# Four output tiles of the seventh image set among the eighth image's norm instead of its energies, in an attention kernel on one core

## The chip, the cores and the metric

The kernel runs on one core of one Trainium2 chip. The metric is the device time of the whole program in microseconds, the median of several runs. The engines are TensorE (PE, matmuls), VectorE (DVE), ScalarE (ACT), GpSimd (POOL) and SyncE (SP, which only issues DMAs here).

## What is computed

The input `x` holds 8 images of 32 x 32 tokens with 256 channels, in float32. Two layers are added to it, each on a group norm without weights (32 groups of 8 channels, mean and variance over the image and the group):

```
x = x + L0(gn(x))        # 8 heads of 32; attention within each row of 32 tokens; projection and bias
x = x + L1(gn(x))        # one head over all 1024 tokens of an image

L1:  q = x Wq, k = x Wk   (256 -> 32)      v = x Wv   (256 -> 256)
     energy = k q^T       (1024 x 1024)    attn = softmax(energy, rows)
     L1 = gamma * (attn v)
```

## The kernel before

Work is told by image. Stage `a` is L0 (norm, q, k, v, scores within windows, softmax, output, projection), stage `b` is L1. A float32 operand is carried as a high and a low float16 half, and a product is three matmuls (high by high, high by low, low by high: `split3`, L274 to L276).

Stage `b` of an image has these steps. The norm (`transposes`, `group_mean`, `group_var`, `group_scale`, then `normalise` on ScalarE and `b_norm_split` on VectorE, which makes the halves) is followed by q and k (`b_project_qk`, L561), whose halves are stacked by four DMAs (`b_stacks`, L332). `b_energy(it)` (L581) computes 128 rows of energies into the two PSUM banks `pb[0]` and `pb[1]`, and `b_maximum` (L1032) takes their row maxima. Energy `it` waits for maximum `it - 1`, since the banks are the same. With all eight maxima there, `b_max_split`, `b_max_rows` and `b_rows_in` put them into the stacks, and `b_energy_T(jt)` (L600) computes the transposed energies less the maximum, again in `pb[0:2]`. ScalarE takes the exponential (L832, L833) and VectorE makes its low half (`b_exp_low`, L1044, semaphore `b_el`). An output tile `b_output(it)` (L611) sums over the eight `jt` the product of exponentials and `v`: 24 matmuls of 257 columns, of which the last column is the sum of the row. `b_factor` (L1051, two small instructions) makes the tile's factor from that sum, `b_scaled` (L835) scales the tile into `y_part`, which has two places and shares its memory with `qk_h`, `b_add` (L1243) adds it to the residual, and `store_pair` (L296) stores two tiles at a time.

The order is written out by hand for every engine, as two half steps per image, `first(i)` and `second(i)`, run one after the other by `all_steps` (L236); images 2 to 4 are a hardware loop, and the others are written out with plain integers. An engine takes its instructions strictly in this order, and a semaphore wait holds up all that is queued behind it on that engine.

- `first(i)` holds on TensorE the outputs of image `i - 1` (L632), eight tiles, and among them the energies of image `i`, and stage `a` of later images where there is one. For i = 7 there is no such image, so it holds the outputs of image 6 and the energies of image 7 alone.
- `second(i)` holds the transposed energies of image `i` and, where they exist, the output projection and the norm and q/k of image `i + 1` (L663).
- The last image is already treated apart (`last_image`, L278): its outputs 0 to 5 are computed `jt` by `jt` inside `second(7)` (`outputs_behind`, L654), into six banks, and only tiles 6 and 7 are left for `first(8)`, which reuse the banks of tiles 0 and 1 and so wait for their scaling (`b_part`).
- `result_bank` (L281) says which bank a tile uses. Images other than the last use `pb[2]` and `pb[3]` in turn, so that tile `it` waits until tile `it - 2` was scaled. The banks `pa[0:4]` belong to stage `a`.
- On VectorE (L1058) each `b_factor` of image `i - 1` stands among the maxima of image `i`. In `second` (L1086) the instructions of the norm's `group_mean` are followed by `b_exp_low(i, 7)`, and that by `group_scale`.

Of the kernel before, what the change touches and what calls it, by code (L numbers as in the profile page):

```python
# [36 lines left out]
IMAGES, TOKENS, CH = 8, 1024, 256  # L37
# [14 lines left out]
def nth(b, per, n):  # L52
    return b * per + n


def build(nc, x, w_qkv, w_proj, b_proj, wq1, wk1, wv1, gamma, ident_d, group_d, masks_d, out):
# [3 lines left out]
    with ExitStack() as ctx:  # L60
# [81 lines left out]
        pa = ctx.enter_context(nc.psum_tensor("pa", [P, 4, CHUNK], F32))  # L142
# [39 lines left out]
        a_ol = sem("a_ol")  # L182
# [95 lines left out]
        def last_image(b):  # L278
            return isinstance(b, int) and b == IMAGES - 1

        def result_bank(b, it):  # L281

            if last_image(b):
                it = it % 6
                return pa[:, it, :] if it < 4 else pb[:, it - 2, :]
            return pb[:, 2 + it % 2, :]

        def out_banks(g):
# [118 lines left out]
        def _(pe):  # L407
# [50 lines left out]
            def a_project_qk(b, c, ds):  # L458
                for d in ds:
                    pe.wait_ge(n_["a"]["nl"], nth(b, 4, 2 * c + 2))  # L460


                    if c == 0 and image(b, 1):
                        pe.wait_ge(a_sub, 1 + d // 2)
                    elif c == 0:
                        after(pe, a_ol, nth(b, 2, 0))
                    elif d < 2:
                        pe.wait_ge(a_qe, nth(b, 4, d + 1))
                    elif isinstance(b, int) and b < 2:
                        pe.wait_ge(a_ke, nth(b, 4, d - 1))  # L470
                    else:
                        pe.wait_ge(a_x1, nth(b, 4, d - 3))
                    project_T(pa[:, d, :], wqkv_h, wqkv_l, slice(d * P, (d + 1) * P), c, a_nh, a_nl).then_inc(a_qk, 1)
# [126 lines left out]
            def b_energy_T(b, jt):  # L600

                if jt == 0:
                    pe.wait_ge(b_rows, nth(b, 1, 1))
                else:
                    pe.wait_ge(b_exp, nth(b, 8, jt))
                for c in range(CHUNKS):
                    last = nc.tensor.matmul(pb[:, c, :], q_stack[0:98, jt * P:(jt + 1) * P],  # L607
                                            k_stack[0:98, c * CHUNK:(c + 1) * CHUNK], start=True, stop=True)
                last.then_inc(b_st, 1)

            def b_output(b, it, b_next, jts=range(TILES)):  # L611

                if last_image(b):
                    pe.wait_ge(b_el, nth(b, 8, jts[-1] + 1))

                    if it >= 6:
                        pe.wait_ge(b_part, nth(b, 8, it - 5))
                elif jts[0] == 0:
                    pe.wait_ge(b_el, nth(b, 8, 8))

                    if it >= 2:
                        pe.wait_ge(b_part, nth(b, 8, it - 1))
                    else:
                        pe.wait_ge(b_vl, nth(b, 4, 4))
                rows = slice(it * P, (it + 1) * P)
                for jt in jts:
                    last = split3(result_bank(b, it)[:, 0:CH + 1], (e_h[:, jt, rows], e_l[:, jt, rows]),
                                  (v_h[:, jt, 0:CH + 1], v_l[:, jt, 0:CH + 1]), start=(jt == 0), stop=(jt == TILES - 1))
                if jts[-1] == TILES - 1:
                    last.then_inc(b_pv, 1)  # L630

            def first(i, b, o, m, f):  # L632

                for it in range(4):
                    if o and not last_image(i - 1): b_output(i - 1, it, b, range(0, 4))
                    if b and it == 2: b_energy(i, 1, m)
                    if o and not last_image(i - 1): b_output(i - 1, it, b, range(4, 8))
                    if f and it == 1: transposes("a", i + 2, range(4))
                    if b and it >= 1: b_energy(i, (0, 2, 3)[it - 1], m)
                for it in range(4, 8):  # L640
                    if o and last_image(i - 1):

                        if it >= 6: b_output(i - 1, it, b)
                        continue
                    if o: b_output(i - 1, it, b, range(0, 4))
                    if m and it == 5: a_output(i + 1, f, 0)
                    if f and it == 5: group_var("a", i + 2)
                    if m and it == 6: a_output(i + 1, f, 1)
                    if b and it == 7: b_energy(i, it, m)
                    if o: b_output(i - 1, it, b, range(4, 8))  # L650
                    if b and it < 7: b_energy(i, it, m)
                    if f and it == 4: group_mean("a", i + 2)

            def outputs_behind(b, jts):  # L654

                for jt in jts:
                    if jt == 0:

                        pe.wait_ge(b_vl, nth(b, 4, 4))
                    for it in range(6):  # L660
                        b_output(b, it, False, (jt,))

            def second(i, b, o, m, f):  # L663
                if b and not image(i, 0): b_project_v(i, (0,))
                if b: b_max_rows(i)
                if b and not image(i, 0): b_project_v(i, (1,))
                if b: b_energy_T(i, 0)
                if b and not image(i, 0): b_project_v(i, (2,))
                if f: a_project_qk(i + 2, 0, (0,))
                if b: b_energy_T(i, 1)  # L670
                if f: a_project_qk(i + 2, 0, (1,))
                if b and not f: b_project_v(i, (3,))
                if b: b_energy_T(i, 2)
                if f: a_project_qk(i + 2, 0, (2, 3))
                if b: b_energy_T(i, 3)
                if f: a_project_qk(i + 2, 1, (0,))
                if last_image(i): outputs_behind(i, (0,))
                if b: b_energy_T(i, 4)
                if b and f and not image(i, 0): b_project_v(i, (3,))
                if last_image(i): outputs_behind(i, (1,))  # L680
                if f: a_project_qk(i + 2, 1, (1,))
                if b: b_energy_T(i, 5)
                if last_image(i): outputs_behind(i, (2,))
                if m: a_projection(i + 1, f, (0, 1))
                if b: b_energy_T(i, 6)
                if last_image(i): outputs_behind(i, (3,))
                if m: a_projection(i + 1, f, (2,))
                if m: transposes("b", i + 1, (0, 1))
                if m: a_projection(i + 1, f, (3,))
                if b: b_energy_T(i, 7)  # L690
                if last_image(i): outputs_behind(i, range(4, 8))
                if f: a_project_qk(i + 2, 1, (2,))
                if f: a_project_qk(i + 2, 1, (3,))
                if m: transposes("b", i + 1, (2, 3))
                for j in range(4):
                    if m and j == 2: group_var("b", i + 1)
                    if f: a_project_v(i + 2, (j,))
                    if m and j == 0: group_mean("b", i + 1)
                if f: a_scores(i + 2)
                for c in range(CHUNKS):  # L700
                    if m: b_project_qk(i + 1, f, c)
# [228 lines left out]
        def _(dve):  # L930
# [126 lines left out]

            def first(i, b, o, m, f):  # L1058
                if m: a_maximum(i + 1, 1)
                if o: b_factor(i - 1, 0)  # L1060
                if m: a_row_sum(i + 1, 0)
                if b: b_maximum(i, 0)
                if o: b_factor(i - 1, 1)
                if m: a_row_sum(i + 1, 1)
                if b: b_maximum(i, 1)
                if o: b_factor(i - 1, 2)
                if m: a_transpose(i + 1, 0)
                if b: b_maximum(i, 2)
                if f: stats("a", i + 2, (0,))
                if b: b_maximum(i, 3)  # L1070
                if o: b_factor(i - 1, 3)
                if f: stats("a", i + 2, (1,))
                if m: a_transpose(i + 1, 1)
                if f: group_mean("a", i + 2)
                if o: b_factor(i - 1, 4)
                if b: b_maximum(i, 4)
                if f: group_scale("a", i + 2)
                if b: b_maximum(i, 5)
                if o: b_factor(i - 1, 5)
                if b: b_maximum(i, 6)  # L1080
                if o: b_factor(i - 1, 6)
                if b: b_maximum(i, 7)
                if b: b_max_split(i)
                if o: b_factor(i - 1, 7)
# [239 lines left out]
```

## Time and profile before

| | |
|---|---|
| median of 3 runs | 681.19 us (679.55 to 682.06) |
| the profiled execution, its own time | 680.34 us |
| its span, first to last instruction | 678.6 us |
| mean granted clock of TensorE | 0.947 of full |
| `second(6)` in it, by TensorE's first value projection to the last q/k matmul | 570.02 to 611.43 us |
| `first(7)` | 611.43 to 638.53 us |
| `second(7)` | 638.53 to 668.64 us |
| `first(8)`, the tail | 668.64 us to the end |

All times in rows are from the start of the span. The duration of a row for a matmul includes its way through the array; one matmul of a dense sequence starts long before the last has ended, so its price is the distance between starts. The granted clock (PEclk) is the mean in a stretch, as a share of 2.4 GHz; 0.50 is 1.2 GHz.

### The profile page before, as it was taken

How to read it: one execution, taken by the hardware profiler on the slowest of the kernel's cores; microseconds unless marked ns; L12 is line 12 of the kernel's file. 1: busy time of each engine (PE TensorE's matmuls, PEld its weight loads, DVE VectorE, ACT ScalarE, POOL GpSimd, SP SyncE). 2: the span in 40 equal slices, each digit the busy share in tenths (PEclk: the TensorE clock that was granted, in tenths of full speed). 3: DMA queues.
4: the chain of work that ended last, by engine and by line, in shares of the span. 5: the costliest groups of instructions: out<-in, count | busy, mean ns of one | idle time of the engine just before them, and what ended most of it. 6: DMA issues, size and time to landing. Idle time of an engine off the chain costs nothing.

```text
span 678.6 us, 15147 instructions
## 1 busy us (share of the span) xinstructions
PE 594.0 (88%) x5859; PEld 429.7 (63%) x5859; DVE 474.0 (70%) x765; ACT 349.0 (51%) x486; POOL 196.3 (29%) x194
## 2 busy tenths in 40 slices
PE   2797827699999999999999999999999999649987
PEld 2464714347776686767775777578676767427756
DVE  4553387567877888687868786887869784764562
ACT  2762233466438751885358643865188514641463
POOL 6432050403244204503351324321450242001303
PEclk8799878779999999999999999999999999779989
DMA  5222413034132232233224313223323132201101
GB/s 165 75 48 65 125 62 86 1 78 108 27 95 78 63 103 72 68 82 94 63 68 108 93 24 93 81 68 90 79 67 75 33 78 68 66 1 39 49 0 63
DMA packets 40308, 47.53 MB, mean 70 GB/s; under 512 B 6848, under 2 KB 32320, under 8 KB 40256
## 3 DMA queue, kind: packets, MB, share of 16 engines
q1 hardware_dynamic: 35792, 42.42, 23.9%
q10 hardware_dynamic: 4464, 4.39, 1.9%
q8 instruction: 35, 0.57, 0.4%
q14 instruction: 17, 0.14, 0.1%
HBM read 10.09 MB, written 8.39 MB: 27 GB/s over the span
## 4 chain that ended last, share of the span: by engine, by line
PE 67%; DVE 16%; ACT 7%; issue 5%; DMA 2%; SPq 2%; POOL 0%; DVEq 0%; ACTq 0%; POOLq 0%
PE pb L274 10%; PE pb L275 9%; PE pb L276 9%; PE pa L274 6%; PE pa L276 6%; PE pa L275 6%; PE pa L541 5%; PE pb L607 4%; DVE max_neg L1034 4%; PE pa L508 4%; PE pb L589 3%; PE pa L429 2%; DVE ast L936 2%; ACT e L833 2%; DVE bst L936 2%
## 5 line engine op out<-in xcount | busy, mean ns | idle before, releaser
L274 PE MATMUL pb<-v_h,e_h 128*128 128x257 f16 x464 | 127.4, 275 | 0.0
L276 PE MATMUL pb<-v_h,e_l 128*128 128x257 f16 x464 | 126.4, 272 | 0.0
L275 PE MATMUL pb<-v_l,e_h 128*128 128x257 f16 x464 | 126.1, 272 | 0.0
L1034 DVE TENSOR_REDUCE max_neg<-pb 128x1 f32<-128x1024 f32 x64 | 77.5, 1211 | 53.6 <-PE pb L589 53.2
L1049 DVE TENSOR_TENSOR e_l<-e,e_h 128x1024 f16<-128x1024 f32 x64 | 77.9, 1224 | 21.1 <-ACT e L833 19.6
L842 ACT ACTIVATE qk_h<-pb,y_fac 128x256 f32<-128x256 f32 x58 | 27.5, 474 | 109.9 <-DVE y_fac L1056 109.6
L1248 POOL TENSOR_TENSOR y<-qk_h,y 128x256 f32<-128x256 f32 x64 | 46.3, 726 | 117.7 <-ACT qk_h L842 117.6
L833 ACT ACTIVATE e<-pb,f_energy 128x1024 f32<-128x1024 f32 x64 | 71.3, 1114 | 16.7 <-PE pb L607 16.7
L1229 POOL TENSOR_TENSOR xb<-xin,bias 128x2048 f32<-128x2048 f32 x8 | 36.2, 4527 | 142.3 <-DVE x L1014 138.9
L1234 POOL TENSOR_TENSOR before_turn<-before_turn,a_rinv 128x1024 f32<-128x1024 f32 x16 | 30.7, 1922 | 93.0 <-DVE a_rinv L995 93.0
L832 ACT ACTIVATE e_h<-pb,f_energy 128x1024 f16<-128x1024 f32 x40 | 44.5, 1114 | 21.3 <-PE pb L607 21.3
L274 PEld LDWEIGHTS pb<-v_h,e_h 128*128 128x128 f16 x464 | 45.7, 99 | 13.6 <-issue 1.4
L275 PEld LDWEIGHTS pb<-v_l,e_h 128*128 128x128 f16 x464 | 45.6, 98 | 11.9
L589 PE MATMUL pb<-q_stack,k_stack 96*128 96x512 f16 x128 | 39.9, 394 | 15.0 <-DVE max_neg L1034 13.0
L274 PE MATMUL pa<-a_nh,wqkv_h 128*128 128x512 f16 x128 | 49.4, 386 | 2.7 <-DVE wqkv_l L1157 1.3
L607 PE MATMUL pb<-k_stack,q_stack 98*128 98x512 f16 x128 | 40.3, 397 | 10.9 <-ACT e L833 9.5
L276 PE MATMUL pa<-a_nh,wqkv_l 128*128 128x512 f16 x128 | 49.2, 385 | 0.0
L275 PE MATMUL pa<-a_nl,wqkv_h 128*128 128x512 f16 x128 | 49.2, 385 | 0.0
L276 PEld LDWEIGHTS pb<-v_h,e_l 128*128 128x128 f16 x464 | 44.6, 96 | 6.9
L1222 POOL TENSOR_TENSOR a_nl<-a_xT,a_nh 128x512 f16<-128x512 f32 x32 | 37.3, 1165 | 23.5 <-ACT a_xT L779 23.5
L777 ACT ACTIVATE a_nh<-a_xT,anb,ar 128x512 f16<-128x512 f32 x32 | 25.7, 804 | 32.8 <-POOL anb L1211 32.8
L541 PE MATMUL pa<-diag,v_tok 128*32 128x128 f32 x1024 | 33.4, 286 | 4.4 <-DMA diag<-turned 4.0
(152 smaller groups left out, 1376.5 us busy)
## 6 DMA issues: line engine op xcount, KB each, us to landing
diag<-qkT SPq DMA_DIRECT2D x64, 128.0 KB, 2.4
diag<-turned SPq DMA_DIRECT2D x64, 128.0 KB, 2.4
xin<-in_x SPq DMA_DIRECT2D x15, 512.0 KB, 4.8
turned<-before_turn SPq DMA_DIRECT2D x120, 64.0 KB, 2.0
out<-y SPq DMA_DIRECT2D x24, 256.0 KB, 2.1
out<-y ACTq DMA_DIRECT2D x8, 256.0 KB, 2.1
q_stack<-qk_hl SPq DMA_DIRECT2D x8, 128.0 KB, 2.3
k_stack<-qk_hl SPq DMA_DIRECT2D x8, 128.0 KB, 2.3
```

The source lines that it names most:

```text
L274: nc.tensor.matmul(out_ap, lh, rh, start=start, stop=False)
L275: nc.tensor.matmul(out_ap, lh, rl, start=False, stop=False)
L276: return nc.tensor.matmul(out_ap, ll, rh, start=False, stop=stop)
L541: last = nc.tensor.matmul(pa[32 * r:32 * r + 32, 2 * g + c, col:col + P].rearrange("p (w q) -> p w q", w=4), v_tok[:, t, h * DH:(h + 1) * ...
L589: last = nc.tensor.matmul(pb[:, c, :], k_stack[0:96, it * P:(it + 1) * P], q_stack[0:96, c * CHUNK:(c + 1) * CHUNK], start=True, stop=True)
L607: last = nc.tensor.matmul(pb[:, c, :], q_stack[0:98, jt * P:(jt + 1) * P], k_stack[0:98, c * CHUNK:(c + 1) * CHUNK], start=True, stop=True)
L832: nc.scalar.activation(e_h[:, jt, :], src, ACT.Exp, scale=f_energy[:, 0:1])
L833: nc.scalar.activation(e32[:, jt % 2, :], src, ACT.Exp, scale=f_energy[:, 0:1]).then_inc(b_exp, 1)
L1034: nc.vector.tensor_reduce(max_neg[:, it:it + 1], pb[:, 0:2, :].rearrange("p a n -> p (a n)"), X, ALU.max, negate=True).then_inc(b_max, 1)
L1049: nc.vector.tensor_tensor(e_l[:, jt, :], e32[:, jt % 2, :], e_h[:, jt, :], ALU.subtract).then_inc(b_el, 1)
L1222: nc.gpsimd.tensor_tensor(a_nl[:, ct, cols], a_xT[:, ct, cols], a_nh[:, ct, cols], ALU.subtract).then_inc(n_["a"]["nl"], 1)
L1248: nc.gpsimd.tensor_tensor(y[:, it, :], y_part[:, it % 2, :], y[:, it, :], ALU.add).then_inc(b_y, 1)
```

## The change

Image 6 gets a treatment like the last image's. Its tiles 0 to 3 go to the banks `pa[0:4]`, which stage `a` no longer needs once image 7's L0 projection is done, and they are computed in `second(6)`: tiles 0 and 1 for `jt` = 0 to 3 behind the transposed energies 3 to 6, for `jt` = 4 to 6 behind the last transposes of the norm, for `jt` = 7 behind `group_mean`; tiles 2 and 3 for `jt` = 0 and 1 right behind that, ahead of `group_var`, and for `jt` = 2 to 7 behind `group_var`, ahead of `b_project_qk`. Each waits for its own low half of the exponentials. `first(7)` keeps tiles 4 to 7, half a tile at a time ahead of each energy. VectorE makes the factors of tiles 0 to 3 at once at the start of `first(7)` and those of 4 to 6 each one place sooner than the same tile had. The tiles 6 and 7 of the last image go to `pb[0:2]`, and wait for its last exponential instead of for the scaling of its tiles 0 and 1.

```diff
         def result_bank(b, it):
 
             if last_image(b):
-                it = it % 6
-                return pa[:, it, :] if it < 4 else pb[:, it - 2, :]
+                return pa[:, it, :] if it < 4 else pb[:, (it - 2) % 4, :]
+            if next_to_last(b) and it < 4:
+                return pa[:, it, :]
             return pb[:, 2 + it % 2, :]
...
@@ b_output (PE)
                     pe.wait_ge(b_el, nth(b, 8, jts[-1] + 1))
 
                     if it >= 6:
-                        pe.wait_ge(b_part, nth(b, 8, it - 5))
+                        pe.wait_ge(b_exp, nth(b, 8, 8))
+                elif next_to_last(b) and it < 4:
+                    pe.wait_ge(b_el, nth(b, 8, jts[-1] + 1))
+                elif next_to_last(b):
+                    if it >= 6:
+                        pe.wait_ge(b_part, nth(b, 8, it - 1))
...
@@ first (PE)
                 for it in range(4):
-                    if o and not last_image(i - 1): b_output(i - 1, it, b, range(0, 4))
+                    if o and b and not next_to_last(i - 1): b_output(i - 1, it, b, range(0, 4))
+                    if next_to_last(i - 1): b_output(i - 1, 4 + it // 2, b, range(it % 2 * 4, it % 2 * 4 + 4))
                     if b and it == 2: b_energy(i, 1, m)
-                    if o and not last_image(i - 1): b_output(i - 1, it, b, range(4, 8))
+                    if o and b and not next_to_last(i - 1): b_output(i - 1, it, b, range(4, 8))
...
-                    if o: b_output(i - 1, it, b, range(0, 4))
+                    if next_to_last(i - 1): b_output(i - 1, 4 + it // 2, b, range(it % 2 * 4, it % 2 * 4 + 4))
+                    elif o: b_output(i - 1, it, b, range(0, 4))
...
-                    if o: b_output(i - 1, it, b, range(4, 8))
+                    if o and not next_to_last(i - 1): b_output(i - 1, it, b, range(4, 8))
...
-            def outputs_behind(b, jts):
+            def outputs_behind(b, jts, its=range(6)):
 
                 for jt in jts:
                     if jt == 0:
 
                         pe.wait_ge(b_vl, nth(b, 4, 4))
-                    for it in range(6):
+                        pe.wait_ge(a_ol, nth(IMAGES, 2, 0))
+                    for it in its:
                         b_output(b, it, False, (jt,))
...
@@ second (PE)
                 if last_image(i): outputs_behind(i, (0,))
+                if next_to_last(i): outputs_behind(i, (0,), (0, 1))
                 if b: b_energy_T(i, 4)
...
                 if last_image(i): outputs_behind(i, (1,))
+                if next_to_last(i): outputs_behind(i, (1,), (0, 1))
...
                 if last_image(i): outputs_behind(i, (2,))
+                if next_to_last(i): outputs_behind(i, (2,), (0, 1))
                 if m: a_projection(i + 1, f, (0, 1))
                 if b: b_energy_T(i, 6)
                 if last_image(i): outputs_behind(i, (3,))
+                if next_to_last(i): outputs_behind(i, (3,), (0, 1))
...
                 for j in range(4):
+                    if next_to_last(i) and j == 0: outputs_behind(i, (4, 5, 6), (0, 1))
                     if m and j == 2: group_var("b", i + 1)
                     if f: a_project_v(i + 2, (j,))
                     if m and j == 0: group_mean("b", i + 1)
+                    if next_to_last(i) and j == 0:
+                        outputs_behind(i, (7,), (0, 1))
+                        outputs_behind(i, (0, 1), (2, 3))
+                    if next_to_last(i) and j == 2: outputs_behind(i, range(2, 8), (2, 3))
...
@@ first (DVE)
+                early = o and next_to_last(i - 1)
                 if o: b_factor(i - 1, 0)
+                if early:
+                    for it in (1, 2, 3):
+                        b_factor(i - 1, it)
...
-                if o: b_factor(i - 1, 1)
+                if o and not early: b_factor(i - 1, 1)
                 if m: a_row_sum(i + 1, 1)
                 if b: b_maximum(i, 1)
-                if o: b_factor(i - 1, 2)
+                if o: b_factor(i - 1, 4 if early else 2)
...
                 if b: b_maximum(i, 3)
-                if o: b_factor(i - 1, 3)
+                if o: b_factor(i - 1, 5 if early else 3)
...
-                if o: b_factor(i - 1, 4)
+                if o and not early: b_factor(i - 1, 4)
...
                 if b: b_maximum(i, 5)
-                if o: b_factor(i - 1, 5)
+                if o: b_factor(i - 1, 6 if early else 5)
                 if b: b_maximum(i, 6)
-                if o: b_factor(i - 1, 6)
+                if o and not early: b_factor(i - 1, 6)
                 if b: b_maximum(i, 7)
                 if b: b_max_split(i)
                 if o: b_factor(i - 1, 7)
```

`next_to_last(b)` is true for image 6 alone.

## Rows read from the trace of the kernel before

**Rows 1.** The page: TensorE's busy time, and its granted clock in 40 slices.
```profile
PE 594.0 (88%) x5859; PEld 429.7 (63%) x5859; DVE 474.0 (70%) x765; ACT 349.0 (51%) x486; POOL 196.3 (29%) x194
...
PEclk8799878779999999999999999999999999779989
```

**Rows 2.** Busy time by stretch: length, PE, PEld, DVE, ACT, POOL, PEclk, DMA.
```profile
570.02:611.43 41.41, 26.74 (x166) 16.89 (x164) 29.65 (x46) 24.89 (x31) 5.63 (x8) 0.79 0.12 32
611.43:638.53 27.10, 26.74 (x221) 20.96 (x219) 13.04 (x27) 4.40 (x9) 5.07 (x7) 1.00 0.15 44
638.53:668.64 30.11, 26.32 (x206) 19.81 (x206) 15.69 (x23) 17.75 (x20) 3.69 (x6) 0.94 0.03 10
```

**Rows 3.** Instructions in order of time, TensorE in second(6): start, duration, [idle before <-releaser].
```profile
600.29 0.38 PE L436 MATMUL pb<-bmv,group_avg 128*128 128x2 f32 x2 [2.80 <-DVE bmv L942]
601.51 0.59 PE L441 MATMUL pb<-be,group_avg 128*128 128x2 f32 x2 [0.84 <-DVE be L954]
606.87 0.61 PE L274 MATMUL pb<-b_nh,wqk_h 128*128 128x512 f16 x1 [4.77 <-DVE b_nl L971]
```

**Rows 4.** The chain that ended last, single matmuls: start, what each adds.
```profile
607.48 0.43 PE pb L275
...
649.14 0.22 PE pa L275
...
660.98 0.11 PE pa L275
```

**Rows 5.** Busy time by stretch, for the granted clock (columns as in rows 2).
```profile
587.00:590.00 3.00, 3.00 (x15) 2.06 (x15) 1.23 (x2) 2.12 (x2) 0.00 (x0) 0.50 0.00 0
591.00:597.00 6.00, 5.49 (x47) 4.44 (x45) 5.00 (x7) 4.17 (x6) 0.00 (x0) 1.00 0.00 0
...
601.00:606.00 5.00, 0.59 (x2) 0.50 (x2) 2.96 (x8) 2.25 (x4) 0.89 (x2) 0.50 0.00 0
...
645.70:648.00 2.30, 0.00 (x0) 0.00 (x0) 2.27 (x3) 2.30 (x3) 0.00 (x0) 1.00 0.00 0
649.00:651.00 2.00, 2.00 (x11) 1.42 (x10) 1.83 (x3) 0.92 (x1) 0.00 (x0) 0.50 0.00 0
```

**Rows 6.** Instructions in order of time, VectorE, from the variance to qk_hl.
```profile
601.38 1.22 DVE L1049 TENSOR_TENSOR e_l<-e,e_h 128x1024 f16<-128x1024 f32 x1
602.51 0.15 DVE L959 TENSOR_SCALAR bve<-pb 128x2 f32<-128x2 f32 x1
...
608.25 0.69 DVE L971 TENSOR_TENSOR b_nl<-b_xT,b_nh 128x512 f16<-128x512 f32 x1
...
612.26 0.75 DVE L1023 SCALAR_TENSOR_TENSOR qk_hl<-qk_h,masks,pb 128x512 f16<-128x512 f16 x1 [1.17 <-ACT qk_h L813]
```

**Rows 7.** Instructions in order of time, TensorE: energies 0, 1, 7, turned energy 0, tail.
```profile
617.01 0.60 PE L589 MATMUL pb<-q_stack,k_stack 96*128 96x512 f16 x2
...
619.02 0.38 PE L589 MATMUL pb<-q_stack,k_stack 96*128 96x512 f16 x1
...
635.37 0.38 PE L589 MATMUL pb<-q_stack,k_stack 96*128 96x512 f16 x1
...
640.39 0.60 PE L607 MATMUL pb<-k_stack,q_stack 98*128 98x512 f16 x2
...
668.64 0.27 PE L274 MATMUL pa<-v_h,e_h 128*128 128x257 f16 x1
```

**Rows 8.** Instructions in order of time, ScalarE, end of first(7) and tail.
```profile
637.94 0.48 ACT L842 ACTIVATE qk_h<-pb,y_fac 128x256 f32<-128x256 f32 x1 [1.94 <-DVE y_fac L1056]
638.64 0.60 ACT L820 ACTIVATE v_h<-pb 128x512 f16<-128x512 f32 x1 [0.22 <-PE pb L276]
639.26 1.02 ACT L824 ACTIVATE k_stack<-pb 2x1024 f16<-2x1024 f32 x1
...
667.59 0.84 ACT L842 ACTIVATE qk_h<-pa,y_fac 128x256 f32<-128x256 f32 x2 [4.56 <-DVE y_fac L1056]
```

**Rows 9.** The page, costliest groups: GpSimd's adds of tiles.
```profile
L1248 POOL TENSOR_TENSOR y<-qk_h,y 128x256 f32<-128x256 f32 x64 | 46.3, 726 | 117.7 <-ACT qk_h L842 117.6
```

More of the change, by code:

```diff
@@ L279, in last_image, with next_to_last @@
             return isinstance(b, int) and b == IMAGES - 1
+        def next_to_last(b):
+            return isinstance(b, int) and b == IMAGES - 2
         def result_bank(b, it):
             if last_image(b):
-                it = it % 6
-                return pa[:, it, :] if it < 4 else pb[:, it - 2, :]
+                return pa[:, it, :] if it < 4 else pb[:, (it - 2) % 4, :]
+            if next_to_last(b) and it < 4:
+                return pa[:, it, :]
             return pb[:, 2 + it % 2, :]
```

## The prediction

> **What bounds the kernel now.** I read the page's totals first: TensorE (PE) is busy 88% of the span, and its clock is granted in full through the whole middle of the run, with weak slices near the start and again in the last seventh [rows 1]. So I went to busy time by stretch for the part that the diff touches [rows 2]. `second(6)`, the first row, is the stretch of 41.41 us in which the eighth image (index 7) gets its output projection, norm and q/k, and the seventh (index 6) its turned energies and exponentials; PE is busy for 26.74 of it, at a mean clock of 0.79. `first(7)`, 27.10 us, holds all eight outputs of image 6 and the eight energies of image 7: PE is busy for 26.74 of 27.10, so PE alone sets its length. VectorE (DVE), which takes the maxima, is busy for less than half. So outputs stand where PE is full, and ahead of them lie some 14 us without PE work, in holes behind ScalarE's exponentials and behind the statistics (2.80 us), the variance (0.84) and the normalisation (4.77) [rows 3]. That is the trade which the change tries.
>
> **Prices.** One matmul of an output tile (257 columns) follows the last at 0.11 us at the full clock (2.4 GHz) and at 0.22 us at the half clock (1.2 GHz); a 512-column matmul takes 0.43 at the half clock [rows 4], and so half of that, 0.22, at the full one. A tile is 24 matmuls: 2.65 us, or 5.2.
>
> **Part 1: four tiles leave first(7), and energies pace it.** 96 matmuls, 10.6 us of PE, go. What is late next? Each energy waits for the maximum of the one before, since both use the same two banks: from energy 0 to energy 1 took 2.01 us with half a tile (1.33) and an energy (0.44) in it [rows 7], with the maximum closing the circle. The new order puts at most half a tile in front of each energy, so 2.0 us is the new pace and PE's 1.77 hides under it. Seven steps are 14.0 us, where energies 0 to 7 took 635.37 - 617.01 = 18.36 us [rows 7]. That is -4.4. Tiles 6 and 7 need a free bank (tiles 4 and 5 scaled). Those factors come behind maxima 1 and 3 and are early by two energies; at the old place the first would still be in time, so this reordering is worth 0 here.
>
> The four factors made at once on DVE are 1.3 us or so (each two tiny operations) and lie in the 4 us in which DVE waits for the stacks' DMAs, so they cost 0. They let ScalarE and GpSimd work off tiles 0 to 3 at 0.73 us a tile [rows 9] from the end of q/k (y_part shares its memory with qk_h, so not before), done about 3.5 us later and hidden under that same wait. SP issues the stores of image 6 earlier, but behind the four stack DMAs; POOL has nothing else ahead of the tail. Both 0, with up to 0.3 us if the stores slow the last stack.
>
> **Part 2: the clock at the first energy.** Before, tiles 0 and 1 filled PE from the end of q/k to energy 0. Now only tile 4 does (2.65 us of 5.2), so PE is idle for some 2.5 us just ahead of energy 0. In second(7) an idle stretch of 2.30 us was followed by a clock of 0.50 [rows 5], so I take the half clock here: energy 0 and the 12 matmuls behind it last 0.86 + 12 x 0.214 = 3.4 us instead of 2.0. That is +1.4 (bounds 0 and +2.4, if the second pair is slow too).
>
> **Part 3: from energy 7 to the first turned energy.** It took 640.39 - 635.37 = 5.02 us [rows 7]: last maximum, split, last factor, scaling at 637.94, value copy, rows copied in at 639.26 [rows 8]. Half a tile no longer stands behind energy 7, so the value projection is there when ScalarE comes to it; 0.70 us between scaling and value copy shrinks to the 0.4 between two scalings in the tail [rows 8]. The rest is a chain of DVE and ScalarE that stays: -0.3.
>
> **Part 4: what second(6) pays.** (a) Tiles 0 and 1, energies 0 to 3: four lots of 6 matmuls. The first two fill holes behind exponentials. The 24 projection matmuls before ran at the half clock until about 590.4 (the row 587 to 590 shows 0.50 with PE full, the row 591 to 597 1.00 [rows 5]); with holes filled, the clock should be back some 3 us sooner, which halves 3.2 us of projections (-1.6) against two lots in the full part (+1.3): -0.3. (b) 18 matmuls (energies 4 to 6) go into the 2.80 us hole: 2.0, hidden. (c) The one that costs: six matmuls of energy 7 and twelve for tiles 2 and 3 are queued **ahead of group_var**, and the first waits for e_l(7), which DVE makes only after it has handed over the variance. e_l(7) ran 601.38 to 602.60, and the scale that closes the variance stood right behind it at 602.51 [rows 6], although PE's part was done before. Now PE starts 18 matmuls at 602.6 - 0.3 = 602.3, ends at 604.3, then does group_var; the scale comes at 604.5: **+2.0**, passed on in full to normalisation, low halves and q/k, since each waits for the one before. (d) 36 matmuls (4.0 us) stand between group_var and the q/k projections. They end near 608.5; the second low half, which let q/k start at 606.87 [rows 3], now comes at 608.9. Hidden by 0.4 us only. (e) q/k ran at the half clock, 12 x 0.43, because PE had been idle in 601 to 606 [rows 5]. Now PE is full up to it. From the last low half (608.94) to the end of qk_hl (613.01) were 4.07 us [rows 6]; with six matmuls at 0.22 it is 1.3 + 0.2 + 0.6 + 0.75 + gaps = 2.95: **-1.1** (bounds -1.1 and 0). Sum of part 4: +0.9 (from -0.3 to +3): energy 0 moves from 617.01 to 617.9, with 4.0 us from qk_hl over the stacks' DMAs unchanged.
>
> Here a rule speaks against the change. The row first: PE idle around 601 to 606 went with 0.50, and 2.3 us idle did so at 648. In the new order PE works 2 us from 596, then nearly idles 3.3 us until e_l(7) comes. The Trainium skill ("TensorE: Matmul & The Clock Gate", section "HAM oscillation — how this bites in real kernels") says that waits between bursts of matmuls bring the half clock back again and again, each burst then starting slow. By that rule the 18 matmuls would take 3.9 us and not 2.0. I keep 2.0 in the sum, because PE did 2 us of work in front of this wait and a group matmul in it; the rule is a rival below.
>
> **Part 5: the tail.** Tile 6 of image 7 waited for tile 0's scaling. It starts at 668.64, on the heel of the matmul before [rows 7], while both first scalings had ended at 668.43 [rows 8]. The wait removed was not waited for: 0. Nothing else in second(7) changes.
>
> **Sum.** Part 4 +0.9, part 1 -4.4, part 2 +1.4, part 3 -0.3: **-2.4 us**. Against the profiled execution (680.34 us, span 678.6) that is 677.9; that execution lies 0.85 below the median of 681.19, so the forecast for a median is **678.8**. A measurement of this kernel can tell about 0.5%, 3.4 us, from no change, and -2.4 is under that.
>
> **Rivals.**
> A, *the clock holds ahead of energy 0.* Tile 4 and q/k before it may be enough work, or the stacks land as the clock would fall. Part 2 goes: -3.8, 677.4. For it: q/k and tile 4 are now dense; against: the 2.3 us idle of [rows 5]. 0.22.
> B, *the half clock behind e_l(7)*, the skill's rule: the 18 matmuls ahead of group_var at 0.214 instead of 0.11: +1.9 on the sum, -0.5, 680.7. For it: [rows 5]; against: the work just ahead. 0.16.
> C, *slower: the block of 36 ahead of q/k becomes the bound.* It has 0.4 us of room. If the clock is low from e_l(7) through the block, group_var ends at 606.2, the block takes 7.7 us to 613.9, and the 12 q/k matmuls another 2.6 to 616.5, against 612.3 in the forecast: +4.2, in sum +1.8, 683.0. It decides once the block starts later than 605 or runs below the full clock. Full work brought the clock back between 590 and 591 [rows 5], so 0.05.
> D, *nothing moved that counts*: energies already wait for the maxima where PE looks full. Rows 2 speak against it (26.74 of 27.10). 681.2, 0.05.
>
> **How the numbers follow.** The forecast case has 0.52. Runs before spread over 2.5 us, and the clock's places shift from run to run, so I take 676.9 (A with half a microsecond) to 681.3 (B, D and spread); C is left out with a part of A's low end. Faster by over 0.5% needs 677.8 or less: A and a little of the forecast case, 0.25. Slower by over 0.5% needs 684.6: the worse half of C, 0.04. Within: 0.71.
>
> **What would show it.** Right: DVE's scale of the variance some 2 us later, with PE full just ahead of group_var; q/k at the full clock; idle PE for 2 to 3 us before the first energy and a clock of 0.5 behind it; energies 2.0 us apart; the same tail from the last turned energy on. Wrong: energies still near 3 us apart, a q/k projection waiting behind outputs, or a tail shorter than before.

## The result, and the profile after

| | before | changed |
|---|---|---|
| median, 5 runs each on one chip | 682.06 us (679.55 to 685.73) | 678.14 us (676.46 to 679.77) |
| ratio, 95% interval | | 0.994 (0.9913 to 0.9967) |
| profiled execution, its span | 680.34, 678.6 us | 676.46, 674.7 us |
| TensorE's mean granted clock | 0.947 | 0.958 |

A second set of 10 runs of the changed kernel gave 678.2 us and a ratio of 0.9957 (0.9929 to 0.9984). The change makes the kernel some 3 to 4 us faster; the forecast was 2.4. In the experiments, one slow run of `var_first` (1025.9 us) and one of `pad_after` (689.25 us) count in the medians and not in the ratios.

The page of the changed kernel. One of 40 slices is 17 us: the one from 645 us on, in `second(7)`, rose from 8 to 9, the two of `second(6)` from 7 and 7 to 8 and 9, and a new 8 stands at the first energy of image 7 [rows 1]:

```profile
PE 589.8 (87%) x5859; PEld 425.7 (63%) x5859; DVE 473.3 (70%) x765; ACT 348.6 (52%) x486; POOL 196.2 (29%) x194
...
PEclk9799878779999999999999999999999999898999
```

Busy time by stretch, columns as in [rows 2]. From the top: second(6), first(7), second(7), then single places for the clock, which are q/k with the end of the block ahead of it, the idle ahead of energy 0, energy 0, the idle ahead of turned energy 3, and what follows that:

```profile
570.28:612.60 42.32, 34.47 (x262) 24.80 (x261) 29.65 (x46) 24.98 (x31) 5.62 (x8) 0.96 0.12 32
612.60:635.20 22.60, 18.00 (x125) 12.08 (x123) 12.10 (x23) 3.80 (x8) 5.01 (x7) 0.92 0.18 53
635.20:664.75 29.55, 25.10 (x206) 19.01 (x205) 16.33 (x28) 18.21 (x21) 3.75 (x6) 1.00 0.03 11
...
606.00:612.00 6.00, 4.92 (x35) 3.05 (x34) 4.84 (x9) 3.52 (x5) 0.01 (x1) 1.00 0.00 0
615.60:618.10 2.50, 0.00 (x0) 0.00 (x0) 0.00 (x0) 0.95 (x2) 2.33 (x4) 0.94 0.70 173
618.20:621.20 3.00, 3.00 (x13) 1.80 (x14) 1.23 (x1) 0.00 (x0) 0.00 (x0) 0.50 0.40 141
643.30:645.60 2.30, 0.00 (x0) 0.00 (x0) 2.27 (x3) 2.30 (x3) 0.00 (x0) 1.00 0.00 0
646.00:648.00 2.00, 1.91 (x17) 1.47 (x16) 1.97 (x3) 1.11 (x1) 0.00 (x0) 1.00 0.00 0
```

`second(6)` is 0.9 us longer with four tiles more in it, `first(7)` 4.5 us shorter, and TensorE no longer fills it. The last two rows are the ones that I had not foreseen: after the same idle ahead of turned energy 3 of image 7 (2.38 us by its own row, of which the stretch holds 2.30) the clock stays full, where it was 0.50 before [rows 5].

TensorE in order of time (energies are L593, turned energies L611 here): the start of the 18 matmuls behind e_l(7), group_var, q/k, energies 0, 1, 2 and 7, turned energies 0 and 3, tile 6's start and the last output matmul:

```profile
602.48 0.28 PE L274 MATMUL pa<-v_h,e_h 128*128 128x257 f16 x1 [1.98 <-DVE e_l L1070]
...
604.48 0.28 PE L445 MATMUL pb<-be,group_avg 128*128 128x2 f32 x2
...
609.16 0.39 PE L274 MATMUL pb<-b_nh,wqk_h 128*128 128x512 f16 x1 [0.42 <-DVE b_nl L992]
...
618.20 0.61 PE L593 MATMUL pb<-q_stack,k_stack 96*128 96x512 f16 x1 [2.78 <-DMA k_stack<-qk_hl]
...
621.42 0.38 PE L593 MATMUL pb<-q_stack,k_stack 96*128 96x512 f16 x1
...
623.43 0.38 PE L593 MATMUL pb<-q_stack,k_stack 96*128 96x512 f16 x1 [1.41 <-DVE max_neg L1055]
...
633.43 0.38 PE L593 MATMUL pb<-q_stack,k_stack 96*128 96x512 f16 x1
...
638.06 0.39 PE L611 MATMUL pb<-k_stack,q_stack 98*128 98x512 f16 x1
...
645.67 0.60 PE L611 MATMUL pb<-k_stack,q_stack 98*128 98x512 f16 x2 [2.38 <-ACT e L854]
...
664.65 0.27 PE L276 MATMUL pb<-v_h,e_l 128*128 128x257 f16 x1
664.76 0.27 PE L274 MATMUL pb<-v_h,e_h 128*128 128x257 f16 x1
...
669.95 0.27 PE L276 MATMUL pb<-v_h,e_l 128*128 128x257 f16 x1
```

The difference of the two spans, piece by piece. The start of turned energy 3 of image 6, ahead of all that is changed, is the zero (582.27 before, 582.53 now); the last output matmul of the kernel before started at 673.83. This is one profile of each kernel.

| piece | before | changed | difference | forecast |
|---|---|---|---|---|
| start to the zero | 582.27 | 582.53 | +0.26 | 0 |
| zero to energy 0 | 34.74 | 35.67 | +0.93 | +0.9 |
| energy 0 to energy 7 | 18.36 | 15.23 | -3.13 | -3.0 |
| energy 7 to turned energy 0 | 5.02 | 4.63 | -0.39 | -0.3 |
| turned energy 0 to the last output matmul | 33.44 | 31.89 | -1.55 | 0 |
| from there to the end | 4.77 | 4.75 | -0.02 | 0 |
| sum | 678.6 | 674.7 | -3.90 | -2.4 |

### The profile page after: what moved, and what is told of

The parts are those of the page before. It is cut to its first block, busy times and chain, and to the rows that moved or that the text cites. A ratio compares the mean times of both kernels' runs of the same rounds, so it can differ in the third digit from the quotient of the medians.

```text
span 674.7 us, 15141 instructions
## 1 busy us (share of the span) xinstructions
PE 589.8 (87%) x5859; PEld 425.7 (63%) x5859; DVE 473.3 (70%) x765; ACT 348.6 (52%) x486; POOL 196.2 (29%) x194
## 4 chain that ended last, share of the span: by engine, by line
PE 64%; DVE 17%; ACT 6%; issue 5%; SPq 4%; DMA 3%; POOL 0%; DVEq 0%; ACTq 0%; POOLq 0%
PE pb L274 9%; PE pb L275 9%; PE pb L276 9%; PE pa L274 6%; PE pa L275 6%; PE pa L276 6%; DVE max_neg L1055 5%; PE pa L545 4%; PE pb L611 4%; PE pb L593 4%; PE pa L512 3%; DVE ast L957 2%; PE pa L433 2%; DVE bst L957 2%; ACT e L854 2%
## 5 line engine op out<-in xcount | busy, mean ns | idle before, releaser
L274 PE MATMUL pb<-v_h,e_h 128*128 128x257 f16 x448 | 123.5, 276 | 0.0
L276 PE MATMUL pb<-v_h,e_l 128*128 128x257 f16 x448 | 122.4, 273 | 0.0
L275 PE MATMUL pb<-v_l,e_h 128*128 128x257 f16 x448 | 122.1, 273 | 0.0
L854 ACT ACTIVATE e<-pb,f_energy 128x1024 f32<-128x1024 f32 x64 | 71.3, 1113 | 15.2 <-PE pb L611 15.2
L593 PE MATMUL pb<-q_stack,k_stack 96*128 96x512 f16 x128 | 40.3, 398 | 19.7 <-DVE max_neg L1055 14.4
L274 PEld LDWEIGHTS pb<-v_h,e_h 128*128 128x128 f16 x448 | 44.3, 99 | 13.3 <-issue 1.7
L275 PEld LDWEIGHTS pb<-v_l,e_h 128*128 128x128 f16 x448 | 44.2, 99 | 11.8 <-issue 0.3
L611 PE MATMUL pb<-k_stack,q_stack 98*128 98x512 f16 x128 | 40.0, 395 | 8.5 <-ACT e L854 7.1
```

The lines of the kernel that those rows point to most:

```text
L274: nc.tensor.matmul(out_ap, lh, rh, start=start, stop=False)
L275: nc.tensor.matmul(out_ap, lh, rl, start=False, stop=False)
L276: return nc.tensor.matmul(out_ap, ll, rh, start=False, stop=stop)
L593: last = nc.tensor.matmul(pb[:, c, :], k_stack[0:96, it * P:(it + 1) * P], q_stack[0:96, c * CHUNK:(c + 1) * CHUNK], start=True, stop=True)
L854: nc.scalar.activation(e32[:, jt % 2, :], src, ACT.Exp, scale=f_energy[:, 0:1]).then_inc(b_exp, 1)
```

## The experiments

All medians are of 5 to 10 runs, with a ratio to the kernel before on the same chip; its medians there lay between 681.2 and 682.0. Since runs spread by several microseconds, the pieces of the profiles carry the verdicts, and each kernel below has one profile. Here they are for all kernels; the diffs and expectations follow. "E0", "E7" are energies 0 and 7 of image 7, "T0" its turned energy 0. The last column is the place of its turned energy 3: how long after turned energy 3 of image 6, the zero, it starts (65.78 in the first profile of before, 63.14 in that of the changed kernel).

| kernel | median | ratio (95%) | zero to E0 | E0 to E7 | E7 to T0 | T0 to last output | place |
|---|---|---|---|---|---|---|---|
| before_again | 681.39 | 1.0016 (0.9992, 1.0039) | 34.29 | 18.37 | 5.02 | 33.36 | 65.34 |
| tail_only | 681.57 | 1.0011 (0.9985, 1.0038) | 34.32 | 18.36 | 5.02 | 33.36 | 65.36 |
| after_again | 678.2 | 0.9957 (0.9929, 0.9984) | 35.63 | 15.21 | 4.63 | 31.90 | 63.09 |
| old_factors | 686.66 | 1.0072 (1.004, 1.0104) | 35.57 | 21.04 | 4.63 | 33.41 | 68.85 |
| var_first | 678.89 | 0.9951 (0.9925, 0.9977) | 34.08 | 16.11 | 4.62 | 33.32 | 62.43 |
| fill_hole | 676.69 | 0.9921 (0.9895, 0.9947) | 37.28 | 14.01 | 4.63 | 31.90 | 63.53 |
| two_early | 676.8 | 0.9933 (0.9909, 0.9956) | 34.80 | 14.01 | 5.03 | 33.59 | 61.50 |
| fill_and_var | 677.08 | 0.9926 (0.9894, 0.9958) | 37.98 | 14.01 | 4.63 | 31.91 | 64.24 |
| two_var | 677.99 | 0.9935 (0.9911, 0.9959) | 34.26 | 14.02 | 5.02 | 33.62 | 60.96 |
| pad_before | 681.63 | 1.0006 (0.998, 1.0032) | 34.37 | 18.37 | 5.76 | 31.90 | 66.12 |
| pad_after | 682.2 | 0.9995 (0.9967, 1.0023) | 39.12 | 15.33 | 7.90 | 33.26 | 70.19 |

**The two kernels once more** (no edit).

> The changed kernel once more, unedited. In the first profile of it the stretch from the first turned energy of image 7 to the last output tile was 1.5 us shorter than before, and the clock did not fall in it. Theory (chance of when the clock falls against the program): a second profile differs in this stretch by about 1.5 us in some runs, while second(6) and first(7) repeat within 0.3 us apart from half-clock pieces. Rival (the change itself keeps the clock up there): the stretch repeats at the short length.

> The kernel before, unedited, profiled a second time. In its first profile second(7), from the first turned energy of image 7 to the last output matmul, took 33.4 us with 3.4 us of half clock in it; two profiles of the changed kernel took 31.9 without. Theory 1 (the shift of the program against the clock's own beat decides, and repeats from run to run): 33.4 again, with the fall at the same place within half a microsecond. Theory 2 (chance from run to run): 31.9 to 33.4, either.

From the zero on, the pieces repeat within 0.1 us, apart from 0.45 in the first one of before: its first profile has 34.74 there, its three relatives 34.3 to 34.4, so that part 4 cost 1.3 us against those and not 0.9. The start up to the zero does not repeat (582.5 and 584.9 in the changed kernel). The short second(7) came again in the changed kernel (31.89, 31.90) and the long one in the kernel before (33.44, 33.36, and 33.36 in tail_only). So it looks like no matter of chance from run to run, which was my first theory.

**Shifting second(7) in time.** In `b_max_split`, for the last image alone, with 1 (pad_before) or 2 (pad_after) repetitions:

```diff
+                if last_image(b):
+                    for k in range(1):
+                        nc.vector.tensor_reduce(wmax[:, k:k + 1], pb[:, 0:2, :].rearrange("p a n -> p (a n)"), X, ALU.max, negate=True)
```

> The kernel before, with one idle-making instruction more: VectorE repeats the last maximum of image 7 into an unused place (1.13 us) ahead of the split of the maxima, so that all of second(7) starts 1.1 us later against the beginning of the program. Theory 1 (the fall of the clock in second(7) is decided by where the idle stretch ahead of turned energy 3 lies in the program's time): from the first turned energy to the last output matmul 31.9 us instead of 33.4, so that the kernel with 1.1 us more work is 0.4 us faster or the same. Theory 2 (chance, or the idle's length alone): still 33.4, and 1.1 us slower.

> The changed kernel with two such maxima (2.3 us), which puts second(7) back to nearly the place in time that it had in the kernel before. Theory 1: the clock falls again in second(7), which takes 33.4 us instead of 31.9, and the kernel is 3.8 us slower than the changed one (about 682). Theory 2: 31.9 stays and it is 2.3 us slower.

pad_before: the idle stretch and what follows it, and the same in pad_after (columns as in [rows 2]):

```profile
646.80:649.10 2.30, 0.00 (x0) 0.00 (x0) 2.27 (x3) 2.30 (x3) 0.00 (x0) 1.00 0.00 0
650.00:652.00 2.00, 2.00 (x19) 1.74 (x18) 1.94 (x3) 0.93 (x1) 0.00 (x0) 1.00 0.00 0
```

```profile
651.30:653.50 2.20, 0.00 (x0) 0.00 (x0) 2.17 (x3) 2.20 (x3) 0.00 (x0) 0.90 0.00 0
654.00:656.00 2.00, 2.00 (x10) 1.22 (x9) 1.54 (x3) 1.11 (x1) 0.00 (x0) 0.50 0.00 0
```

Both stretches came out as theory 1 has it: with 1.1 us of useless work the kernel before loses the fall and is not measurably slower, and with 2.3 us the changed kernel gets it back. By medians it is 4.0 us slower than the changed kernel, by the two ratios 2.6 (3.8 expected). But the pads did not move the stage as planned. pad_before moved it by only 0.3 to 0.8 us against the profiles of before. pad_after did not bring it back to its old place but to 4.4 us behind that. Most of the excess, 3.5 us, arose ahead of the pad, in instructions that are the same as in the changed kernel, and so from run to run: the half clock behind turned energy 3 of image 6 lasted until 8.3 us behind the zero instead of 4.6 (+1.8), and the 18 matmuls behind e_l(7) ran at it too (3.66 us instead of 2.00). The rest is an idle of 2.68 us on TensorE behind the pad, with the half clock after it, hence the 7.90.

What carries the theory is all 13 profiles in the order of their place. The idle ahead of turned energy 3 is 2.38 us in each of them. The clock fell behind or in it at 60.96, 61.50 and 62.43; it stayed full at 63.09, 63.14, 63.53 and 64.24; it fell at 65.34, 65.36 and 65.78, stayed full at 66.12, and fell at 68.85 and 70.19. var_first and the changed kernel have the same instructions from q/k on, and 0.7 us in place between them. So neither the idle's length nor the edit decides, and the place orders the outcomes; that nothing else which comes with the place does it is not shown.

**VectorE's factors at their old places.** By the code, factor 4 stands behind maximum 1 in the changed kernel and behind maximum 3 here, factor 5 behind maxima 3 and 5, factor 6 behind 5 and 6: the first two had moved by two maxima, not by one place.

```diff
-                early = o and next_to_last(i - 1)
+                early = False
```

> TensorE as changed, VectorE's factors of image 6 at their old places. The prediction (step: reordering worth 0) expects the same time as the changed kernel. Rival: the first half of tile 6 stands ahead of energy 4 and waits for the scaling of tile 4, whose factor now comes only behind maximum 3. Then the loop energy 3, maximum 3 (ends 1.85 us after it), factors 3 and 4, scaling (0.5), half a tile (1.33), energy 4 takes about 4.5 us instead of 2.0, and the same happens again between energies 5 and 6 with tile 7 (4.2 instead of 2.0): +4.7 us on the changed kernel, about 0.6 us above the kernel before.

TensorE's waits in first(7) of this kernel (in all, how many, the longest), and what VectorE does between maxima 3 and 4:

```profile
PE pb L274 <- ACT qk_h L863: 4.7, 3, 2.5
PE pb L593 <- DMA k_stack<-qk_hl: 2.8, 1, 2.8
PE pb L593 <- DVE max_neg L1055: 1.4, 1, 1.4
```

```profile
627.43 1.22 DVE L1055 TENSOR_REDUCE max_neg<-pb 128x1 f32<-128x1024 f32 x1 [0.78 <-PE pb L593]
...
628.76 0.16 DVE L1077 TENSOR_TENSOR y_fac<-y_inv,f_out 128x1 f32<-128x1 f32 x1
...
629.04 0.16 DVE L1077 TENSOR_TENSOR y_fac<-y_inv,f_out 128x1 f32<-128x1 f32 x1
633.24 1.23 DVE L1055 TENSOR_REDUCE max_neg<-pb 128x1 f32<-128x1024 f32 x1 [4.05 <-PE pb L593]
```

The first row is the wait of tiles 6 and 7 for a scaled bank (2.46 and 2.09 us) and a short one of the value projection. Factor 4 comes at 629.04, behind maximum 3; the half tile that waits for its scaling stands ahead of energy 4, and maximum 4 starts 5.81 us behind maximum 3 instead of 2.0. Energies 0 to 7 take 5.8 us more than in the changed kernel (4.7 expected; the half tile ran at the half clock behind this wait, 2.56 us to energy 4's start instead of 1.33). With the fall in second(7), that is 7.3 of the 8.5 us between the medians; the rest is left open.

**Only the last image's banks and wait.**

```diff
-                it = it % 6
-                return pa[:, it, :] if it < 4 else pb[:, it - 2, :]
+                return pa[:, it, :] if it < 4 else pb[:, (it - 2) % 4, :]
...
-                        pe.wait_ge(b_part, nth(b, 8, it - 5))
+                        pe.wait_ge(b_exp, nth(b, 8, 8))
```

> The kernel before with only the last image's part of the change: its tiles 6 and 7 in the banks of the turned energies, waiting for the last exponential and not for two scalings. The prediction says 0: tile 6 started with no idle before it already. Rival: the wait cost up to 0.7 us, and the time from the last low half of the exponentials to the end falls by that.

No gain, as predicted: from the start of the last exponential to the last scaling are 12.62 us in both (663.64 to 676.26, and 661.92 to 674.54).

**group_var ahead of the block.**

```diff
-                    if next_to_last(i) and j == 0:
-                        outputs_behind(i, (7,), (0, 1))
-                        outputs_behind(i, (0, 1), (2, 3))
-                    if next_to_last(i) and j == 2: outputs_behind(i, range(2, 8), (2, 3))
+                    if next_to_last(i) and j == 2:
+                        outputs_behind(i, (7,), (0, 1))
+                        outputs_behind(i, range(8), (2, 3))
```

> The 18 matmuls of energy 7 for tiles 0 and 1 and energies 0 and 1 for tiles 2 and 3 go behind group_var instead of ahead of it; nothing else. Theory: the variance's scale comes 2.3 us sooner, right behind e_l(7); q/k then waits for the block of 54 matmuls (6.0 us from 602.5) until about 608.5 instead of starting at 609.2, and its second half for the last low half, so qk_hl and energy 0 come about 1.5 us sooner, and the time falls by 1.5. Rival 1: the block runs at the half clock, since TensorE is idle ahead of it just the same, and becomes the bound: energy 0 comes 1 to 4 us later. Rival 2: nothing but the exponentials' low half matters: 0.

Energy 0 came 1.6 us sooner, right. But the idle ahead of it was the same 2.8 us, and this time the clock fell only 1.1 us behind energy 0's start and came back at 624, so that it slowed three steps (2.35, 2.47 and 3.28 us):

```profile
617.50:623.50 6.00, 4.59 (x19) 2.32 (x18) 3.13 (x5) 0.47 (x1) 0.72 (x1) 0.50 0.02 7
```

Energies 0 to 7 took 0.9 us more, second(7) lay where the clock falls (+1.4), and no gain is left (1.5 us expected).

**Tile 5 into the wait for the stacks.**

```diff
+                if next_to_last(i - 1):
+                    b_output(i - 1, 4, b)
+                    b_output(i - 1, 5, b)
+                    for it in range(8):
+                        b_energy(i, it, m)
+                        b_output(i - 1, 6 + it // 4, b, range(it % 4 * 2, it % 4 * 2 + 2))
+                    return
```

with factor 4 among VectorE's early ones and factor 5 behind maximum 0.

> Tiles 4 and 5 both stand ahead of energy 0, where TensorE was idle for 2.8 us waiting for the stacks, and tiles 6 and 7 follow as a quarter tile behind each energy; VectorE makes factor 4 with the early ones and factor 5 behind maximum 0. Theory (the half clock at energy 0 comes from the idle ahead of it): the clock stays full, energy 0 to energy 1 takes 2.0 us instead of 3.2, the other steps stay at 2.0 since the maxima pace them: -1.2 us on the changed kernel. Rival: with half as much work between energies TensorE is so sparse that the clock falls later in first(7), which costs up to 0.4 us per energy and gives the gain back: 0 to +1.

Stretches of its profile: the block behind e_l(7), and all of the energies:

```profile
603.00:605.50 2.50, 2.50 (x14) 1.88 (x13) 0.16 (x1) 0.00 (x0) 0.59 (x1) 0.50 0.00 0
...
618.80:634.00 15.20, 9.98 (x65) 5.82 (x66) 9.58 (x12) 0.95 (x2) 1.45 (x2) 1.00 0.13 46
```

The clock holds through all energies, and they take 14.01 us: -1.2, as expected, though TensorE is busy for only two thirds of the stretch. So the idle ahead makes the first energy slow in the changed kernel. The others say the same: the four kernels without that idle, or with less than 1 us of it, took 14.01 or 14.02 us wherever energy 0 lay (34.3 to 38.0 behind the zero), and the five profiles with 2.8 us of it took 15.2 or more.

The first row is the prediction's rival B, alive: here the clock fell inside the 18 matmuls ahead of group_var (at 602.6). It fell there in two of the five profiles of kernels with these 18 (fill_hole, pad_after) and not in three (the two of the changed kernel, old_factors). Energy 0 came 1.6 us later than in the changed kernel, but the clock accounts for half of that: qk_hl was done 0.9 us later. The rest is SyncE, which took 1.34 us to issue the third stack DMA:

```profile
615.38 1.34 SPq L345 DMA_DIRECT2D q_stack<-qk_hl  x1
```

It took 1.01 us in fill_and_var, and 0.59 or 0.60 in the other eleven profiles. These two are the kernels with tiles 4 and 5 ahead of energy 0; why it took longer there is not shown.

**Both together, and only two tiles early.** fill_and_var is the sum of the last two edits. two_early moves tiles 0 and 1 alone into second(6) and sets tiles 2 and 3 where fill_hole has 4 and 5, with half a tile behind each energy; two_var also moves the 6 matmuls of energy 7 from ahead of group_var to right ahead of q/k.

```diff
-                        outputs_behind(i, (0, 1), (2, 3))
-                    if next_to_last(i) and j == 2: outputs_behind(i, range(2, 8), (2, 3))
...
+                if next_to_last(i - 1):
+                    b_output(i - 1, 2, b)
+                    b_output(i - 1, 3, b)
+                    for it in range(8):
+                        b_energy(i, it, m)
+                        b_output(i - 1, 4 + it // 2, b, range(it % 2 * 4, it % 2 * 4 + 4))
+                    return
```

> Both fill_hole and var_first. Alone, var_first brought energy 0 1.6 us sooner and lost it again to two steps at the half clock behind a longer idle; here tiles 4 and 5 fill that idle. Theory: energy 0 1.6 us sooner, energies 0 to 7 in 14.0 us, in sum -2.8 us on the changed kernel, about 675.4. Rival: the 54 matmuls behind e_l(7) run in part at the half clock, as in the profile of fill_hole, and hold q/k: the gain shrinks to that of fill_hole (-1.5) or to nothing.

> Only tiles 0 and 1 move into second(6); tiles 2 and 3 fill the wait for the stacks ahead of energy 0, and tiles 4 to 7 follow as half a tile behind each energy; VectorE as in the changed kernel. Theory: the variance waits for 6 matmuls instead of 18 (0.7 us instead of 2.0), but TensorE then idles ahead of q/k, which runs at the half clock as before (+1.1), so energy 0 comes at about the same time as in the changed kernel (within 0.3); no idle stands ahead of it, so energies 0 to 7 take 14.0 us instead of 15.2, and a half tile behind energy 7 costs 0.3: -0.9 us on the changed kernel. Rival: what counts is how much work leaves the energies, and with six tiles left first(7) stays longer: +1 or more.

> two_early with the 6 matmuls of energy 7 for tiles 0 and 1 moved behind group_var, right ahead of q/k, where TensorE idles anyway. Theory: the variance waits for nothing, energy 0 comes 0.7 to 1.2 us sooner than in two_early, all else is the same: about 676.0. Rival: the clock in second(7), which fell in the profile of two_early, decides over more than this (1.5 us either way).

The profile of fill_and_var went the rival's way: 14.01 us for the energies, but the block of 54 matmuls ran partly at the half clock (7.6 us; 6.0 in var_first) and held q/k, and energy 0 came 2.3 us later than in the changed kernel. Up to q/k its instructions are those of var_first, and yet q/k started 3.5 us later after the zero; as in pad_after, the half clock behind turned energy 3 of image 6 had lasted twice as long. So this part differs from run to run. Three of its ten runs took 673.8 to 674.0 us, less than any run of any other kernel here (the next is 675.4). They may be the 675.4 of the theory; without profiles of them that is not shown.

two_early is the cheaper answer. Its q/k ran at the half clock, as before, yet energy 0 came 0.85 us sooner than in the changed kernel (0 to 0.3 expected), and the energies took 14.01 us; energy 7 to turned energy 0 took 0.4 us more (0.3 expected). two_var brought energy 0 another 0.5 us sooner (0.7 to 1.2 expected). Both lie in the fall of second(7) (+1.7), and their medians cannot be told from the changed kernel's nor from fill_hole's: the intervals overlap. All four beat the kernel before; none is shown to beat the changed one.

## Why the prediction was right

- *Part 1, energies paced by maxima at 2.0 us*: from energy 1 on 2.00 or 2.01 us apart. Right.
- *Part 2, the half clock at energy 0*: 3.22 us for the first step, 3.4 predicted, clock 0.50. Right, and fill_hole and the kernels behind it show that the idle ahead makes it.
- *Part 3*: 4.63 us, 4.7 predicted.
- *Part 4a*: -0.3 predicted. group_mean's matmul came 17.59 us behind the zero after 18.02, but the three other profiles with second(6) as before have 17.7 there, so it is -0.1. *4c, group_var behind 18 matmuls*: it started at 604.48, 604.3 predicted. *4d*: q/k waited 0.42 us for the low half behind the block, 0.4 predicted. *4e*: q/k at the full clock, and from the last low half to the end of qk_hl 2.95 us, as predicted.
- *Part 5, the tail*: 0, shown by tail_only.
- *Rival B* was right as a mechanism, and 0.16 looks too little: it did not come in the two profiles of the changed kernel, but in 2 of the 3 others that have the same 18 matmuls there. That the profile of the result had none of it was luck.
- *"Nothing else in second(7) changes"* failed. It is the 1.5 us by which the forecast fell short. No instruction changed there ahead of the tail, but the whole stage came 2.6 us earlier after the zero, and whether the clock falls behind its idle of 2.38 us goes with such a shift, as the thirteen profiles in order of place show. That it went the good way, and not back as in var_first, was luck too; without it the two profiles would differ by 2.35 us, which is the forecast.
- *"This reordering is worth 0"* in part 1 failed too, unseen in the total. I had checked when factor 4 must be there for tile 6 itself, but not that tile 6's first half stands ahead of energy 4 on TensorE, so that the wait closes a loop over maximum 3. The reordering on VectorE carries 5.8 us: without it the change is slower than before. The prediction was made for a kernel that has the reordering, so this error did not touch its sum.

## What to carry to other kernels

When work is put in front of an instruction on an in-order engine, follow the loop that its wait closes: a factor two maxima too late cost more than the whole change brought. Look for an idle stretch that ends in a dense part: here filling 2.8 us of it took 1.2 us off the part behind, all of it clock. Where a stage without any edit gets faster or slower, look at the granted clock in it before looking for a cause in the code: a useless delay of 1.1 us bought back what it cost. And profile more than once: from the zero to energy 0, the same instructions on TensorE took 35.6 to 35.7 us in three profiles and 39.1 in a fourth.

## What the runs showed of the hardware

An idle TensorE stretch of 2.38 us is followed by the full clock (changed kernel at 646, pad_before at 650) or by half of it (before at 649, pad_after at 654), and in unchanged kernels the outcome repeated: 3 of 3 profiles with second(7) at its old place fell, 2 of 2 of the changed kernel did not. Over all 13 profiles the outcome goes with the place of the stretch, and it changes four times between 61 and 70 us behind the zero. The same idle ahead of turned energy 3 of image 6 was followed by the fall in all 13. The Trainium skill ("TensorE: Matmul & The Clock Gate", section "HAM oscillation — how this bites in real kernels") describes bursts that start slow after waits; the traces agree for the idle of 2.78 us ahead of energy 0, and for 2.38 us they show both outcomes. TensorE kept the full clock through 15.2 us in which it was busy for 9.98.
